# One scan of 128x1024 per state in place of four of 128x256, in a fused FFN, state-space and FFN layer

## The reference

```python
# FFN:   hidden = sigmoid(x @ q(w1).T) * (x @ q(w2).T);  out = hidden @ q(w3).T
# state-space layer, 16 states per channel:
xz = einsum('bld,kd->blk', x, W_x)                # 128 dt_raw, 16 B, 16 C
dt = softplus(einsum('blr,dr->bld', dt_raw, W_dt) + b_dt)
d_a = exp(dt[..., None] * a)                      # a = -exp(A_log)
dbx = dt[..., None] * b_ssm[:, :, None, :] * x[..., None]
def step(h, inp):                                 # over the 2048 tokens
    h = da_t * h + dbx_t
    y = einsum('bdn,bn->bd', h, c_t)
y + x * D_param
```

## Time and profile before

| | |
|---|---|
| time, median of 3 runs | 925.68 us (922.63 to 927.62) |
| span of the profiled execution | 922.9 us |
| VectorE busy | 817.9 us (89%) |
| TensorE busy | 681.0 us (74%) |
| GpSimd busy | 591.3 us (64%) |
| ScalarE busy | 566.3 us (61%) |
| stretch of the scans (104 to 874.5 us) | VectorE busy 84.03 of 92.00 us in chunk 0, some 94 of 98 to 99 us in a chunk between |

### The profile page before, as it was taken

One profiled execution on the slowest core, in us unless ns is written; L12 is line 12 of the kernel. 1 busy time (PEld: TensorE's weight loads), 2 busy tenths in 40 slices (PEclk: granted clock), 3 DMA queues, 4 the chain that ended last, 5 costly groups with the idle time before them and its releaser, 6 DMA issues. The chain is left out here.

```text
span 922.9 us, 15428 instructions
## 1 busy us (share of the span) xinstructions
PE 681.0 (74%) x5152; PEld 555.8 (60%) x5152; DVE 817.9 (89%) x1113; ACT 566.3 (61%) x1298; POOL 591.3 (64%) x418
## 2 busy tenths in 40 slices
PE   5566595368986888688986898789769894247568
PEld 4455374157865776567764786578557773035457
DVE  4974999899998999899989998999989998989931
ACT  5413565857587667955795768765885587355232
POOL 0370274776678758866777678876887488637502
PEclk7787797669997999889997998799979998559869
DMA  9300000000001000010001000100000000000000
GB/s 365 89 1 24 0 1 23 1 0 2 1 1 47 1 1 1 10 40 1 2 1 47 1 2 1 47 1 1 1 24 1 1 1 2 23 0 1 23 1 24
DMA packets 15009, 18.82 MB, mean 20 GB/s; under 512 B 3664, under 2 KB 12368, under 8 KB 14928
## 3 DMA queue, kind: packets, MB, share of 16 engines
q1 hardware_dynamic: 14928, 17.80, 5.6%
HBM read 13.60 MB, written 4.19 MB: 19 GB/s over the span
## 5 line engine op out<-in xcount | busy, mean ns | idle before, releaser
L344 PE MATMUL work<-x_hi,q 128*128 128x256 f16 x1408 | 338.0, 286 | 38.9 <-DVE hid L831 20.3
L344 PE MATMUL work<-x_lo,q 128*128 128x256 f16 x1408 | 336.7, 285 | 0.0
L1080 POOL TENSOR_TENSOR shared<-shared 128x1024 f32<-128x1024 f32 x120 | 284.5, 2371 | 60.3 <-DVE shared L902 59.9
L892 DVE TENSOR_TENSOR_SCAN shared<-decay,last_state,shared 128x256 f32<-128x256 f32 x448 | 304.4, 729 | 13.8 <-ACT decay L689 7.3
L689 ACT ACTIVATE decay<-shared,a_neg 128x256 f32<-128x256 f32 x512 | 221.1, 468 | 111.9 <-DVE shared L892 107.4
L1064 POOL TENSOR_TENSOR hid_lo<-hid,hid_hi 128x256 f16<-128x256 f32 x176 | 122.0, 707 | 137.9 <-ACT hid_hi L626 137.1
L344 PE MATMUL work<-hid_hi,q 128*128 128x256 f16 x704 | 162.6, 279 | 38.0 <-POOL hid_lo L1064 18.5
L344 PEld LDWEIGHTS work<-x_hi,q 128*128 128x128 f16 x1408 | 144.7, 103 | 71.8 <-DVE hid L831 25.7
L344 PE MATMUL work<-hid_lo,q 128*128 128x256 f16 x704 | 162.9, 279 | 0.0
L344 PEld LDWEIGHTS work<-x_lo,q 128*128 128x128 f16 x1408 | 144.3, 102 | 23.1
L879 DVE TENSOR_TENSOR shared<-shared,bc_row 128x1024 f32<-128x1024 f32 x128 | 154.9, 1210 | 0.3
(11 more groups left out here) (112 smaller groups left out, 788.2 us busy)
## 6 DMA issues: line engine op xcount, KB each, us to landing
x_in<-xT SPq DMA_DIRECT2D x8, 512.0 KB, 4.0
outT<-x SPq DMA_DIRECT2D x7, 512.0 KB, 3.2
shared<-w1T SPq DMA_DIRECT2D x4, 704.0 KB, 7.0
shared<-w2T SPq DMA_DIRECT2D x4, 704.0 KB, 11.5
shared<-w3T SPq DMA_DIRECT2D x3, 768.0 KB, 13.5
shared<-w3T SPq DMA_DIRECT2D x1, 512.0 KB, 15.2
outT<-x SPq DMA_DIRECT2D x2, 256.0 KB, 2.2
wx<-w_xT SPq DMA_DIRECT2D x1, 256.0 KB, 11.4
```

The lines of the kernel that those rows point to most:

```text
L344: return nc.tensor.matmul(out, lhsT, rhs, start=start, stop=stop)
L892: nc.vector.tensor_tensor_scan(out=states[:, n % HR, k, :], data0=decay[pair][:, j, :], data1=dbx[:, n % 2, k, :], initial=state, op0=ALU. ...
L1080: nc.gpsimd.tensor_tensor(x2[:, par, :, :] if n == NS - 1 else y[:, 0, :, :], x1d[:, par, :, :] if n == 0 else y[:, 0, :, :], prod[:, n % ...
```

## The change: one scan over all four channel tiles

The four tiles lie behind one another in the free dimension, so one scan of 1024 elements runs over all of them. For the tiles not to leak into one another, the decay of the first column of each tile is zero: the exponentials write columns 1 to 255 (`decay[:, n % 2, k, 1:TC]`), and column 0 is set to zero once. The carry from the chunk before is then added to the first column of `dbx`: `carry[:, n, :]` is the true decay of that column times `last_state`. The true decays of the first columns of all 16 states are made once per chunk: one small product on GpSimd in `softplus_tail` (`first_exp`), one exponential of 128x64 on ScalarE at place 150 (`first_decays`), and two small products on GpSimd (`carries`, places 141 and 11 of the next chunk). On VectorE `add_carry` adds four elements per partition behind `times_b` and place 3, in chunks 1 to 7.

`decay` moves to SBUF with two buffers of 128x1024 (`n % 2`), `dbx` to PSUM with one buffer of two banks. The decays of state s + 1 now wait for the scan of state s - 1 only, both pairs stand together ahead of `save_state` and of places 1 and 2, and `times_b` of state s + 1 waits for the scan of state s. The tables keep their numbers and get three entries.

```diff
-    dt_raw=102, z0=111, z1=121, logs=122, square0=131, std0=140, x_hi0=150, d_xln=91, bc_mid=122)
+    dt_raw=102, z0=111, z1=121, logs=122, square0=131, std0=140, x_hi0=150, d_xln=91, bc_mid=122, first_decay=150)
...
-    fold_x0=60, x_lo0=141, bc_rest=120, add_x1=91)
+    fold_x0=60, x_lo0=141, bc_rest=120, add_x1=91, carry_low=141, carry_high=11)
...
-        dbx = carve(2)
...
+        decay = sb("decay", [P, 2, KD, TC])
...
-        decay = [pb(f"decay{i}", [P, 2, TC]) for i in range(2)]
+        dbx = pb("dbx", [P, KD, TC])
...
             waits.wait_ge(sp_tail, 3 * c + 3)
+            if not first(c):
+                engine.tensor_tensor(first_exp[:, :, :], a_neg[:, :, :].rearrange("p k n -> p n k"),
+                                     dt[:, par, :, 0].unsqueeze(1).to_broadcast([P, NS, KD]), ALU.mult).then_inc(first_exp_done, 1)
...
-                if not (isinstance(g, int) and g == 0):
-                    act.wait_ge(scan_done, KD * (g - 1) + 2 * pair + 2)
+                if pair == 0 and not (isinstance(g, int) and g < 2):
+                    act.wait_ge(scan_done, g - 1)
                 for j in range(2):
                     k = 2 * pair + j
-                    ins = nc.scalar.activation(decay[pair][:, j, :], dt[:, par, k, :], ACT.Exp,
+                    ins = nc.scalar.activation(decay[:, n % 2, k, 1:TC], dt[:, par, k, 1:TC], ACT.Exp,
                                                scale=a_neg[:, k, n:n + 1])
                 ins.then_inc(decay_done, 1)
+
+            def first_decays(c):
+
+                act.wait_ge(first_exp_done, c)
+                nc.scalar.activation(first_decay[:, :, :], first_exp[:, :, :], ACT.Exp).then_inc(first_decay_done, 1)
...
                         elif not last(c):
-                                decays(c + 1, 0, 1 - par, pair)
-                        if pair == 0 and s > 0:
-                            save_state(c, s - 1)
-                        elif pair == 0 and not first(c):
-                            save_state(c - 1, NS - 1)
-                        beside_scan(c, par, 10 * s + pair + 1)
+                            decays(c + 1, 0, 1 - par, pair)
+                    if s > 0:
+                        save_state(c, s - 1)
+                    elif not first(c):
+                        save_state(c - 1, NS - 1)
+                    beside_scan(c, par, 10 * s + 1)
+                    beside_scan(c, par, 10 * s + 2)
...
-                if not (isinstance(g, int) and g < 2):
-                    dve.wait_ge(scan_done, KD * (g - 1))
-                nc.vector.tensor_tensor(dbx[:, n % 2, :, :], u[:, par, :, :], bcast(bc_row[(n + 1) % 2][:, 0, :]),
+                if not (isinstance(g, int) and g < 1):
+                    dve.wait_ge(scan_done, g)
+                nc.vector.tensor_tensor(dbx[:, :, :], u[:, par, :, :], bcast(bc_row[(n + 1) % 2][:, 0, :]),
                                         ALU.mult).then_inc(dbx_done, 1)
 
-            def scans(c, n, pair):
+            def add_carry(c, n):
+
                 g = NS * c + n
                 dve.wait_ge(dbx_done, g + 1)
-                dve.wait_ge(decay_done, 2 * g + pair + 1)
-                if pair == 0 and not (isinstance(g, int) and g < HR):
+                if n == 0 or n == NS // 2:
+                    dve.wait_ge(carry_done, 2 * (c - 1) + (1 if n == 0 else 2))
+                nc.vector.tensor_tensor(dbx[:, :, 0], dbx[:, :, 0], carry[:, n, :], ALU.add).then_inc(fix_done, 1)
+
+            def scan(c, n):
+                g = NS * c + n
+                if first(c):
+                    dve.wait_ge(dbx_done, g + 1)
+                else:
+                    dve.wait_ge(fix_done, NS * (c - 1) + n + 1)
+                dve.wait_ge(decay_done, 2 * g + 2)
+                if not (isinstance(g, int) and g < HR):
 
                     dve.wait_ge(state_saved, g - HR + 1)
-                for j in range(2):
-                    k = 2 * pair + j
-                    state = 0.0 if first(c) else last_state[:, n, k:k + 1]
-                    nc.vector.tensor_tensor_scan(out=states[:, n % HR, k, :], data0=decay[pair][:, j, :],
-                                                 data1=dbx[:, n % 2, k, :], initial=state,
-                                                 op0=ALU.mult, op1=ALU.add).then_inc(scan_done, 1)
+                nc.vector.tensor_tensor_scan(out=states[:, n % HR, :, :].rearrange("p k t -> p (k t)"),
+                                             data0=decay[:, n % 2, :, :].rearrange("p k t -> p (k t)"),
+                                             data1=dbx[:, :, :].rearrange("p k t -> p (k t)"), initial=0.0,
+                                             op0=ALU.mult, op1=ALU.add).then_inc(scan_done, 1)
...
                 for s in range(NS):
                     beside_scan(c, par, 10 * s)
-                    scans(c, s, 0)
+                    scan(c, s)
                     beside_scan(c, par, 10 * s + 1)
...
                     beside_scan(c, par, 10 * s + 3)
-                    scans(c, s, 1)
-
+                    if s < NS - 1 and not first(c):
+                        add_carry(c, s + 1)
+                    elif s == NS - 1 and not last(c):
+                        add_carry(c + 1, 0)
...
+            def carries(c, half):
+
+                some = slice(half * NS // 2, (half + 1) * NS // 2)
+                pool.wait_ge(state_saved, NS * (c - 1) + (half + 1) * NS // 2)
+                if half == 0:
+                    pool.wait_ge(first_decay_done, c)
+                nc.gpsimd.tensor_tensor(carry[:, some, :], first_decay[:, some, :], last_state[:, some, :],
+                                        ALU.mult).then_inc(carry_done, 1)
```

More of the change, by code:

```diff
@@ L111, in macaron @@
         last_state = sb("last_state", [P, NS, KD])
+        decay = sb("decay", [P, 2, KD, TC])
+        first_exp = sb("first_exp", [P, NS, KD])
+        first_decay = sb("first_decay", [P, NS, KD])
+        carry = sb("carry", [P, NS, KD])
         wx = sb("wx", [P, KD, RANK])
@@ L203, in macaron @@
         state_saved = sem("state_saved")
+        decay_zeroed, first_exp_done = sem("decay_zeroed"), sem("first_exp_done")
+        first_decay_done, carry_done, fix_done = sem("first_decay_done"), sem("carry_done"), sem("fix_done")
         def ffn1_pass(chunk):
@@ L675, in save_state @@
             def save_state(c, n):
-                act.wait_ge(scan_done, KD * (NS * c + n + 1))
+                act.wait_ge(scan_done, NS * c + n + 1)
                 nc.scalar.activation(last_state[:, n, :], states[:, n % HR, :, TC - 1], ACT.Copy).then_inc(state_saved, 1)
@@ L763, in beside_scan @@
                         softplus_logs(c + 1)
+                    if now == AT_ACT["first_decay"]:
+                        first_decays(c + 1)
                 if not last(c) and not before_last(c):
@@ L896, in times_c @@
             def times_c(c, n, par):
                 g = NS * c + n
-                dve.wait_ge(scan_done, KD * (g + 1))
+                dve.wait_ge(scan_done, g + 1)
                 dve.wait_ge(bc_done, g + 3)
@@ L907, in _ @@
             nc.vector.memset(minus_one[:, :], -1.0)
+            nc.vector.memset(decay[:, :, :, 0:1], 0.0).then_inc(decay_zeroed, 1)
             nc.vector.memset(zero_eps[:, 0:1], LN_EPS)
@@ L1028, in scan_chunk @@
                     beside_scan(c, par, 10 * s + 3)
-                    scans(c, s, 1)
+                    if s < NS - 1 and not first(c):
+                        add_carry(c, s + 1)
+                    elif s == NS - 1 and not last(c):
+                        add_carry(c + 1, 0)
+            dve.wait_ge(decay_zeroed, 1)
             scan_all(dve, scan_chunk)
@@ L1134, in beside_scan @@
                     softplus_tail(pool, nc.gpsimd, c + 1, 1 - par)
+                if not last(c) and now == AT_POOL["carry_low"]:
+                    carries(c + 1, 0)
+                if not first(c) and now == AT_POOL["carry_high"]:
+                    carries(c, 1)
                 if not last(c) and not before_last(c):
```

## The result

The changed kernel takes **954.21 us** (median of 4 runs, 952.93 to 954.51) against 926.33 (4 runs of the kernel before beside them): ratio **1.0306 [1.0283, 1.0329]** (its time over that of the kernel before run beside it, with a 95% interval, here and below), 3.1% slower. The forecast was 932 in a range of 914 to 946. The sign was right, the size was not: +6.2 us of span forecast, +29.5 measured (952.4 against 922.9).

The account below looks back on a forecast made before the run. VectorE bounds each chunk up to `hid2` 8, ScalarE's softplus chain the rest. Chunks sum 1.25 + 7.4 + 0.7 - 2.1 - 1 = +6.2, giving 929.1 us of span; with 2.8 added, 932 us, range 914 to 946.

Parts of the forecast that it names:

- Part one: Chunk start to `hid2` 8, some 73 us, set by VectorE: sum +0.15, and +0.6 more in chunks 1 to 4.
- The scan: VectorE's scan of 1024 elements takes 2.19 us, 0.41 less than four short ones with the pointer.
- Rivals E: The long scan costs four short ones, 2.36, or `times_b` into PSUM 0.1 to 0.2 more: 950 us; chance 10%.
- F: The scan's fixed part is the large one, so a long scan takes 1.4 us: 849 us; chance 2%.
- Own waits: VectorE's waits on the instruction right ahead, eleven up to `hid2` 8: +1.4 us, and 0.1 more for each of six in the loop.
- Rival B: VectorE's waits on the instruction right ahead and the loop's extra are free: 14.2 less, 918 us; chance 8%.
- The stalls behind the removed scans: New VectorE stalls where scans had covered waits: `norm` 2 0.8, `hid1` 6 0.65, `hid2` 0 0.5 us.
- the sum +0.15: the gain is used up: Up to `hid2` 8: scans -4.0, additions +0.8, own waits +1.4, stalls +0.8 +0.65 +0.5, together +0.15 us.
- The softplus part: From `hid2` 8 to the next chunk, 25.9 us, set by ScalarE's softplus chain: 14th scan 0.7 later, sum +1.1.
- Rival C: VectorE alone sets the time: ScalarE reaches `logs` earlier and the 14th scan doesn't wait, 898 us; chance 14%.
- Rival D: The carry comes late through GpSimd and VectorE's addition for state 0 waits, 2 us in seven chunks: 946 us; chance 6%.
- the two signs of being wrong: A chunk's first part 2 us shorter than before, or the part behind `hid2` 8 under 25 us.

Follow-up runs that it names:

- experiments 5: The changed kernel with the reciprocals of norms 2 and 0 one place earlier and TensorE's spread for norm 0 at 143: 945.52 us, ratio 1.0229.
- experiment 7: The changed kernel with `hid1` 5 and 6, `hidden_hi` 5 to 7 and `hidden_lo` 5 and 6 one place later: 944.04 us, ratio 1.0213.
- Experiments 1 and 3: First: the changed kernel with chunks 1 to 4 written out, 944.60 us. Second: the changed kernel, loop kept, with the carry left out, 932.83 us.
- experiment 10: The changed kernel, one scan of 1024, chunks written out, reciprocals earlier, `hidden_hi` 8 and 9 behind `logs`, `hid1` 5 and 6 later: 913.57 us, ratio 0.9876.

## Why the prediction was wrong in size and right in sign

Point by point, for chunk 2, whose rows it used. Part one, from the chunk's first scan to `hid2` 8, took 75.75 us (299.77 to 375.52) against 73.39 before: +2.36, and +0.75 was forecast. My sums over the starts of all rows of that stretch:

| term of part one | forecast | measured |
|---|---|---|
| 13 long scans for 50 short ones | -4.0 | -3.83 |
| 12 `times_b`, the wait of the addition behind them | +0.72 | +0.76 |
| 12 additions with the scans' waits behind them, loop extra included | +2.1 | +2.8 |
| `norm` 2, `hid1` 6, `hid2` 0 | +1.95 | +1.77 |
| decays of state 4 late | none | +0.73 |

The small rest, 0.13, lies spread over the other rows.

- **The scan: right.** 2.20 against 2.19. Rivals E (2.36, or a dearer `times_b` into PSUM, which takes its 1.13 as before where nothing waits for it) and F (1.4 of fixed part) fall. E's 950 us lay near the result by another cause, which is chance. The Trainium skill, "DVE: opcode table, instruction layouts, handler registers and perf-mode slots", section "Datapath and trigger behaviour", has the scan at half throughput: the trace agrees, 2.20 for 1024 elements against 1.11 for `times_c`.
- **Own waits: the kind right, the size in the loop too small.** `times_b` with a wait behind it costs 1.26 in the new rows, 0.12 to 0.13 more than bare; that step held. The scan's wait costs 0.21 from the addition's start when written out (0.20 forecast) and 0.36 to 0.37 in the loop (0.30 forecast). Rival B falls. The Trainium skill, "VectorE: DVE Perf Modes", section "The DRAIN you can't avoid", says that a semaphore after each of eight copies costs nothing extra. No run here has such copies; what costs here is a wait on the instruction right ahead.
- **The stalls behind the removed scans: right in kind and sum.** 0.67, 0.86 and 0.24 for 0.8, 0.65 and 0.5; experiments 5 and 7 take the first two away.
- **The step that failed** is "the sum +0.15: the gain is used up". It counted what the removed scans had hidden on VectorE alone. That the scan now waits for both pairs of decays was weighed only at softplus. It also binds in state 4 (0.7 to 0.8 in six chunks, 1.0 in chunk 0), where `hidden_hi` 7 stands ahead of the decays and waits for VectorE: experiment 7. The sum had this wait at nothing. With the 0.7 by which the additions and waits of the loop were undersized it is most of the 1.6 by which part one came out above its forecast. It is 5.2 of the 23 us that were missed in all, as the account below shows.
- **The softplus part: right.** The 14th scan came 14.46 us behind `hid2` 8 (14.3 forecast), and from there to the next chunk's first scan, without the 4.22, it is 27.19 against 25.89 us: +1.3, and +1.1 was forecast. The sign to look for, four or five us idle ahead of the 14th scan, came differently: 3.58 there, with 0.54 ahead of the scan of state 13 and 1.07 ahead of `centre` 0, and in chunks 3 and 4 only 1.9 and 2.2. Rival C falls: the 14th scan is late in every one of chunks 1 to 6, by 1.9 to 4.2 us (put down to the decays in four of them, to ScalarE's `save_state` and to issue in the others), though its own test, `bc_mid` clearly less than 5 us behind `hid2` 8, was no test: it is 4.66 now and was 4.63 before. Rival D falls: none of VectorE's waits is that of an addition for the carry. Neither of the two signs of being wrong came, so they did not warn of this miss.
- **The loop's branch: not seen at all.** 4.22 us ahead of chunk 3. Experiments 1 and 3 show that it needs both loop and carry.
- **One chunk stood for all.** Chunk 2 of the profile was the slowest of before: 99.28 against 98.46 in two of its like, since its part behind `times_b` 13 was 22.80 and not 22. In chunks 1, 3 and 4 that is 0.8 us, in chunk 5 0.5, by which the kernel before was shorter than the sum had it. The prediction also read "2.3 us and more in a chunk" into the earlier trace rows; one of the four waits, in chunk 4, is 0.45. And of the 2.8 us that it adds to a span only 1.8 lies between the time of a run and its own span (2.1 in the changed kernel); the other 1.0 is spread between runs.

For the missing 23 us (29.3, the table by chunk with chunk 7, less 6.2) that gives, by these rows: the branch 4.2, state 4's decays 0.7 x 6 + 1.0 = 5.2, additions and waits in the loop 0.7 x 4 = 2.8, the chunk that stood for all 0.8 x 3 + 0.5 = 2.9, and 1.2 in state 6 of chunk 5, which came and went between kernels. That is 16.3; the other 6.8 us, in chunks 0, 6 and 7 above all, I have not assigned, which were forecast at -1, +0.7 and -2.1 and came out at +1.3, +2.3 and -0.5.

## What to carry to other kernels

An instruction that is made shorter on the busiest engine, in a kernel whose order was fitted to the old one, is priced twice: by its own duration, and by every wait it used to cover on *all* engines. Here the change is 1.5% in favour where the order suits it, and in the old order the waits turned it into 3.1% against; three moves in the order's tables and the written-out loop took enough of them away (the 14th scan still waits 1.3 to 4.2 us in experiment 10). Before you drop such a change, list the new stalls of one chunk, move what causes each, and run the same moves on the old kernel as a control, since that alone tells whose gain it is. When several instructions become one, what fed them one by one must now all be there at its start: follow the feeding engine's queue ahead of each, not only at its busiest place.

## What was not expected of the hardware

- A VectorE instruction that waits for the one right ahead costs more in the loop, where its wait value comes from registers: 0.36 us from the addition's start to the scan's, 0.21 written out. The loop of the kernel before, which has hardly such waits, costs nothing (ratio 0.9998).
- Where the loop branches back, the scan that waits for an addition issued ahead of the branch started 4.22 us late. Without the carry, or without the loop, it did not. What of the branch takes the time was not tried; a group of four instruction transfers stands at that place.
- The fixed part of a scan of 512 or 1024 elements is small: two of 512 cost 0.04 to 0.05 us more than one of 1024.
